# Causal mask of a ViT layer: GpSimd masks of the probabilities replaced by constant stack rows and 64x64 triangle products on TensorE

## What is computed

```python
q = (x @ wq).reshape(Bx, Sx, N_HEADS, HEAD_DIM)          # x: layernorm of the embedding
k = (x @ wk).reshape(Bx, Sx, N_KV_HEADS, HEAD_DIM)
v = (x @ wv).reshape(Bx, Sx, N_KV_HEADS, HEAD_DIM)
q, k = _apply_rope(q, cos, sin), _apply_rope(k, cos, sin)
# k, v broadcast to 16 heads
scores = jnp.einsum('bshd,bthd->bhst', q, k) * scale
scores = jnp.where(causal[None, None, :, :], scores, jnp.float32(-jnp.inf))
attn = jax.nn.softmax(scores, axis=-1)
out = jnp.einsum('bhst,bthd->bshd', attn, v).reshape(Bx, Sx, Dx)
h = h + out @ wo
```

## Time and profile before

| | us |
|---|---|
| median of 3 runs (lowest to highest) | 851.62 (848.73 to 854.28) |
| the profiled execution's own time | 848.58 |
| its span in the trace | 846.9 |
| TensorE's granted clock, mean | 0.96 of full |

### The profile page before, as it was taken

How to read it: one execution, slowest core, us unless ns; L and a number is a source line. 1 busy time by engine, 2 the same in 40 slices (tenths; PEclk the granted TensorE clock), 3 DMA queues, 4 the chain that set the end, 5 groups by cost and what they waited for, 6 DMA issues and landing times. The chain is left out here.

```text
span 846.9 us, 20521 instructions
## 1 busy us (share of the span) xinstructions
PE 704.5 (83%) x6706; PEld 370.9 (44%) x6706; DVE 725.5 (86%) x1064; ACT 554.0 (65%) x844; POOL 536.9 (63%) x545
## 2 busy tenths in 40 slices
PE   3577998998999999999999999999867289995765
PEld 2343444454544445544444554444322133333443
DVE  5855899998999999999999999998774469997997
ACT  3346677666776777677677767767555178884664
POOL 1446777787777788887778888776643268871000
PEclk9899999999999999999999999999898689997999
DMA  8235666566656555565565556554543122223588
GB/s 271 57 84 113 111 141 128 117 127 120 136 130 136 143 127 115 125 139 132 132 147 127 115 120 139 132 130 94 85 72 82 37 54 47 50 50 99 181 265 249
DMA packets 245638, 102.85 MB, mean 121 GB/s; under 512 B 214496, under 2 KB 240864, under 8 KB 245600
## 3 DMA queue, kind: packets, MB, share of 16 engines
q1 hardware_dynamic: 245600, 102.37, 52.9%
HBM read 33.13 MB, written 16.78 MB: 59 GB/s over the span
## 5 line engine op out<-in xcount | busy, mean ns | idle before, releaser
L1206 DVE TENSOR_REDUCE act_all<-pair 128x4 f16<-128x1024 f32 (+1 forms) x192 | 234.6, 1222 | 31.0 <-PE pair L561 30.4
L991 POOL TENSOR_SCALAR_AFFINE_SELECT act_all<-act_all 128x512 f32<-128x512 f32 x128 | 104.9, 830 | 74.8 <-ACT act_all L852 74.8
L852 ACT ACTIVATE ffn<-pair 128x768 f32<-128x768 f32 x128 | 103.3, 807 | 69.9 <-PE pair L578 69.8
L852 ACT ACTIVATE act_all<-pair 128x768 f32<-128x768 f32 x128 | 104.1, 813 | 58.1 <-PE pair L578 58.1
L508 PE MATMUL pair<-act_all 128*128 128x256 f16 (+1 forms) x960 | 117.2, 276 | 17.5 <-DVE act_all L1253 15.4
L991 POOL TENSOR_SCALAR_AFFINE_SELECT ffn<-ffn 128x512 f32<-128x512 f32 x128 | 86.2, 674 | 64.7 <-ACT ffn L852 64.7
L508 PEld LDWEIGHTS pair<-act_all 128*128 128x128 f16 (+1 forms) x960 | 90.4, 99 | 35.8 <-issue 19.3
L1030 POOL TENSOR_TENSOR act_all<-act_all 128x1280 f16<-128x1280 f32 x31 | 82.2, 2653 | 18.9 <-ACT act_all L807 18.9
L1298 DVE TENSOR_SCALAR act_all<-act_all 128x256 f32 (+1 forms) x64 | 88.4, 1420 | 0.8 <-POOL act_all L1037 0.8
L576 PE MATMUL pair<-act_all 64*128 64x256 f16 x512 | 73.2, 282 | 14.6 <-DMA act_all<-act_all 5.0
L522 PE MATMUL pair<-act_all 128*128 128x384 f16 x384 | 75.3, 333 | 0.1
(11 more groups left out here) (132 smaller groups left out, 1440.5 us busy)
## 6 DMA issues: line engine op xcount, KB each, us to landing
act_all<-x_t SPq DMA_DIRECT2D x32, 640.0 KB, 4.2
out<-act_all SPq DMA_DIRECT2D x32, 256.0 KB, 2.6
ffn<-out SPq DMA_DIRECT2D x16, 512.0 KB, 4.7
out<-ffn SPq DMA_DIRECT2D x16, 512.0 KB, 3.2
act_all<-act_all SPq DMA_TRANSPOSE x192, 2.8
act_all<-w_down SPq DMA_DIRECT2D x1, 704.0 KB, 9.0
act_all<-w_emb SPq DMA_DIRECT2D x1, 640.0 KB, 4.0
ffn<-w_gate SPq DMA_DIRECT2D x1, 640.0 KB, 7.3
```

What stands on the lines that cost most here:

```text
L852: act.activation(probs[i // 4][:, o:o + 2, 0:3, :].rearrange("p h k s -> p h (k s)"), pair[1][:, :].rearrange("p (h c) -> p h c", h=2)[:, ...
L991: pool.affine_select(out=p, in_=p, pattern=[[0, 4], [1, P]], compare_op=ALU.is_ge, fill=0.0, base=0, channel_multiplier=-1).then_inc(maske ...
L1206: dve.tensor_reduce(to, pair[2][:, :].rearrange("p (k g t) -> p k g t", k=2, g=n_), AX.X, ALU.max).then_inc(unit_reduced, 1)
```

## The change

Each score pair gets four more products, which add a 64x64 triangle of `MASKED` to the diagonal blocks of the scores before the exponential. The 64-blocks above the diagonal are pushed down by constants in rows 49 to 63 of both stacks, written once at the start like those of `max_stack`. GpSimd's masks, their views and their semaphore go; `attend` waits for the exps. In `unit_pair` only the first product into a bank carries the start flag.

```diff
-        diagonals = [p.rearrange("p h (a b) s -> p (h a) b s", a=2)[:, :, 0, :] for p in probs]
...
-        masked = sem("masked")
...
                             pe.matmul(max_bank[j][:, g * P:(g + 1) * P], max_op[rows, 0, g, :],
-                                      max_op[rows, 0, 4, :], start=True, stop=False, skip_group_check=True)
+                                      max_op[rows, 0, 4, :], start=(g == 0), stop=False, skip_group_check=True)
...
-                                      max_op[rows, 1, 2 * (p // 2 - 1) + g, :], max_op[rows, :, 4, :], start=True,
+                                      max_op[rows, 1, 2 * (p // 2 - 1) + g, :], max_op[rows, :, 4, :], start=(g == 0),
...
                 for rows, b in zip(halves, st_bank):
-                    pe.matmul(b[:, 0:TOKENS], op[rows, k, 0:P], op[rows, pair_, :], start=True, stop=True)
+                    pe.matmul(b[:, 0:TOKENS], op[rows, k, 0:P], op[rows, pair_, :], start=True, stop=False,
+                              skip_group_check=True)
                 for rows, b in zip(halves, st_bank):
-                    mm = pe.matmul(b[:, TOKENS:3 * P], op[rows, k, P:TOKENS], op[rows, pair_, P:TOKENS],
-                                   start=True, stop=True)
+                    pe.matmul(b[:, TOKENS:3 * P], op[rows, k, P:TOKENS], op[rows, pair_, P:TOKENS],
+                              start=False, stop=False, skip_group_check=True)
+
+                for b in st_bank:
+                    for t in halves:
+                        on_diagonal = b[t, :].rearrange("p (c t) -> p c t", c=4)[:, 0:3:2, t]
+                        mm = pe.matmul(on_diagonal, tri_b[t, t],
+                                       eye_b[t, t].rearrange("p (a t) -> p a t", a=1).to_broadcast([64, 2, 64]),
+                                       start=False, stop=True, skip_group_check=True)
                 mm.then_inc(scored, 1)
...
-                pe.wait_ge(masked, x.n * 8 + (4 * half + 4))
+                pe.wait_ge(exp_done, x.n * PAIRS_S + (4 * half + 4))
...
-            def mask(x, r):
-
-                pool.wait_ge(exp_done, x.n * PAIRS_S + (r + 1))
-                fence(pool)
-                p = diagonals[r // 4][:, 4 * (r % 4):4 * (r % 4) + 4, :]
-                pool.affine_select(out=p, in_=p, pattern=[[0, 4], [1, P]], compare_op=ALU.is_ge,
-                                   fill=0.0, base=0, channel_multiplier=-1).then_inc(masked, 1)
...
-            for block_ in range(TOKENS // 64):
-                at_ = max_stack[64 * (block_ % 2):64 * (block_ % 2) + 64, block_ // 2]
-                if block_ < 3:
-                    dve.memset(at_[:, 0:HEADS, 16 + 5 * block_:21 + 5 * block_], -FAR)
-                if block_ > 0:
-                    dve.memset(at_[:, HEADS:QK, 16:16 + 5 * block_], FAR)
+            for stack_, first in ((max_stack, 16), (stacks[0], 49), (stacks[1], 49)):
+                for block_ in range(TOKENS // 64):
+                    at_ = stack_[64 * (block_ % 2):64 * (block_ % 2) + 64, block_ // 2]
+                    if block_ < 3:
+                        dve.memset(at_[:, 0:HEADS, first + 5 * block_:first + 5 + 5 * block_], -FAR)
+                    if block_ > 0:
+                        dve.memset(at_[:, HEADS:QK, first:first + 5 * block_], FAR)
```

More of the change, by code:

```diff
@@ L1042, in step @@
                 early, late = x + 1, x + -1
-                if (x + -1).exists():
-                    mask(late, 1)
                 if (x + 1).exists():
@@ L1048, in step @@
                     add_rotated(late)
[L1049 to L1052, removed]
                 if (x + 4).exists():
                     x_low(early + 3)
[L1055 to L1060, removed]
                 if (x + 2).exists():
```

## The result

The changed kernel takes 867.8 us in the median (866.5 to 870.4, four runs), beside 851.3 us (848.7 to 854.3, four runs) of the kernel before: ratio 1.020, 95% interval 1.016 to 1.024. Slower, as forecast, whether by more or by less than 2% stays open; 866 was said.

What follows compares the result with a forecast made beforehand. Two nearly full engines, PE and DVE, DVE held by GpSimd. Steps +16.9, head +0.2, tail -2: together +15 on the profiled 848.6, 863.6; with the median 3.0 higher 866.6, said as 866; range 852 to 884.

Steps and rivals of the forecast that it cites:

- Bound: Image step: PE and DVE nearly full, DVE held by GpSimd's L1030; PE has some 16.7 us of work in 18.6.
- Price of a group: Four added 64x64 products per score pair on PE cost 0.225 us, 1.8 us a step, taken from L561.
- The lower bound: Added products on PE: 0.11 us a score pair, if row groups run side by side and the shape change is free.
- the upper one: Added products on PE: 0.38 us a score pair, if the 0.15 of entry comes on top.
- The walk: One image step followed along PE with 0.225 us more per score: the next step starts at 19.35 us.
- The wait of score 7: PE, before score 7: a new wait for exp 6 on ACT, 0.34 us in place of 0.15.
- The relief: Masks gone from GpSimd: L1030 starts about 2.2 us earlier, DVE behind L1298 comes 1.5 us earlier.
- the 0.53 us before unit pair 1: PE's pause before unit pair 1, idle 0.46 and the tail ahead of it; it goes because DVE comes earlier.
- The sum over 26 steps: Steady image pipeline between two L1253: 26 x (19.35 - 18.70) = +16.9 us.
- The base of 18.70: Step time of the kernel before, from L1253 at 90.59 to that at 576.73, 26 steps of 18.70 us each.
- Head: Kernel start: twelve more memsets on DVE, about 1.7 us, mostly covered by a DMA wait: +0.2 us.
- Tail: Last steps: attend no longer waits for masks, 2 us won in each of two, 1 lost in each last two: -2.

Runs made afterwards that it cites:

- The run with both: The changed kernel with GpSimd's eight masks per image put back and attend waiting for them, so products and masks together: 874.3 us, ratio 1.026.
- the doubled kernel: The changed kernel with the four triangle products of each score pair issued twice: 886.8 us, ratio 1.042.
- the new-shape kernel: The changed kernel with four 64x128 triangle products, shaped like the score products, in place of the 64x64 ones, without constant stack rows: 849.6 us, ratio 0.998.

## Why the prediction was right

- *Bound.* Two engines near full, DVE held by GpSimd's L1030: the runs with and without masks 2 to 4 show it. That PE's list sets the step afterwards holds too (PE 97%, and doubling the products shows in the time), but for the 0.47 us behind unit pair 4 in which it still waits for L1240.
- *Price of a group*, 0.225 from L561's row: 0.23. The row of the same form was the right one. The lower bound turned out a real price, of another case: 0.11 is what a group costs in a shape that is already there. No run shows the upper one, 0.38.
- *The walk.* Step 19.35 said, 19.25 measured. The wait of score 7 came where it was put, with exp 6 ending at 9.21 (9.22 said); it is 0.23 us instead of 0.34, since unit pair 0 ends some 0.12 later than said (out_project takes 1.42 us where 1.31 was put in), and the wait on L1253 at the end shrank (7.6 us in 16 steps from 9.6). L1030 ended 5.1 us into the step, as said, but by luck: it started 2.65 us earlier instead of 2.2, and took 0.42 longer. L1298 ended at 5.57, not 6.0, which had no effect.
- *The relief.* Here the step of the argument was weaker than its number. The prediction let the 0.53 us before unit pair 1 go because DVE comes earlier. The run with both shows that the added products alone fill that pause, and that the relief is needed only for 0.24 us before unit pair 2. Nor did all of DVE come 1.5 us earlier: reduction 0 starts 9.30 us into the step (315.11) where it started at 9.74 (308.56), 0.44 earlier, since DVE now waits 0.94 us for ACT's copies into the stack and 0.36 more before `residual`. With both causes present the sum is the same; taken apart, the relief is worth about 0.3 us a step behind the products, and 0.70 without them. That the pause went as forecast is thus in part luck.
- *The sum over 26 steps*: +16.9 said, +14.9 measured; the steps are 19.27 us in the mean instead of 19.35. The base of 18.70 was not a steady step: it holds one of 20.96 us (184.13 to 205.09 on L1253, with a wait of 1.5 us on a transfer and a clock of 0.92 of full). The changed kernel has no such step in its profile; most of the others have one or two there, 0.7 to 1.6 us longer than their steady ones. From steady step to steady step the change costs 0.67 us, 17.4 in 26 steps.
- *Head*: +0.2 said, +2.0 measured. The memsets were sized right: DVE's idle time before 10.99 fell from 1.49 to 0.30 us, PE's first product came 0.34 later, and by 27.6 us nothing of it was left. At the first score the changed kernel was even 0.15 us ahead (65.06 against 65.21). What was missing in the term are the score groups of the first image and a half, which also pay and stand before the first of the 26 steps. How much of the 2.0 is theirs isn't settled: over the twelve traces this L1253 starts between 90.6 and 95.8 us, latest in the kernel without masks and without products.
- *Tail*: -2 said, +0.9 measured. Mis-sized: attend no longer waits for GpSimd, and in the last four steps TensorE's granted clock is 0.91 to 1.00 where it was 0.82 to 0.91, but the won time went to the transfer that out_project needs and to the groups. Over the last five L1253 the two kernels are 0.3 us apart, and 0.6 lie behind the last one. The list of waits of PE from 590 to 681 us, against the earlier trace rows:

```profile
PE pair L623 <- DMA act_all<-ffn: 4.9, 4, 1.8
```

The 4.4 us came back as 4.9. I had followed attend and score 6 through, but not `on_low` and its transpose behind them. Head and tail erred in one direction and the steps in the other: together +17.8 for +15. That the total came so close is in part luck.

## What to carry to other kernels

A small product group has the price of its shape as well as of its columns: look in the time line at what stands before and after it, and put an added group into the shape of its neighbour; here that halved its price and took the change from 2% slower to no slower. When two engines are both near full, work moved from a third one may relieve one of them and load the other: price the two halves apart (one run without the old work and with nothing in its place does it), since the pauses that one half opens may be filled by the other anyway. And an operation on GpSimd costs less by its length than by what it pushes into a VectorE operation behind it.

## What was not expected of the hardware

The two L1298 give way to GpSimd's operation wholly, and it does not give way to them. In the tail of the changed kernel, with GpSimd idle, the pair takes 0.73 us. In the kernel without masks it starts 1.8 us into GpSimd's operation and takes 1.74.

```profile
666.84 0.73 DVE L1285 TENSOR_SCALAR act_all<-act_all 128x256 f32<-128x256 f32 x2
```

```profile
298.88 1.74 DVE L1276 TENSOR_SCALAR act_all<-act_all 128x256 f32 x2
```

```profile
297.07 3.08 POOL L1020 TENSOR_TENSOR act_all<-act_all 128x1280 f16<-128x1280 f32 x1
```

Wherever the pair starts in GpSimd's operation, its first operation ends 0.15 us behind that one's end, and the second, 0.40 us long, follows: the pair takes 1.74, 1.38 and 1.16 us when it starts 1.8, 2.16 and 2.4 us in (the last in the doubled kernel). In the kernel before the first one meets mask 4, and the second, which starts 0.10 us behind L1030, lasts until 0.15 behind its end; hence 3.23. GpSimd pays nothing for this: 2.65 us there, and 2.61 where no VectorE operation of these stands beside it (76.68). Its 3.07 us come with another neighbour, `on_low`:

```profile
307.35 1.08 DVE L1257 TENSOR_TENSOR ffn<-act_all,ffn 128x512 f16<-128x512 f32 x1 [0.63 <-ACT ffn L873]
```

In the nine kernels with 3.07 it still runs when GpSimd's operation starts, and for 0.59 us more; in the three with some 2.65 it has ended 1.6 us before. So in these traces L1298 was held by whatever GpSimd operation ran beside it, also by one that started 0.07 us later (in the kernel with products and masks together), and GpSimd was held by `on_low` alone. No run moved `on_low` by itself.

TensorE's shapes: a pair of 128-column products in the shape of its predecessor costs about 0.055 us (four for 0.11, in the new-shape kernel and for the second four of the doubled group), against 0.23 for four in a shape of their own between two others; 0.10 of the difference is the entry into the shape.
